# Decayed V of an attention block: built in each step from the loaded V instead of ahead of time within the MLP

## The chip, the cores and the metric

The kernel runs on one core of one Trainium2 chip. The metric is the device time of one execution in microseconds, and the median over the runs is compared.

## What is computed

The input is x of shape (4, 512, 512): 2048 tokens of width 512. Cut to what matters:

```
xn = layernorm(x)
q, k, v = xn @ wq.T, xn @ wk.T, xn @ wv.T      # 16 query heads, 4 key and value heads, head size 128
q, k = rope(q), rope(k)
s = lightning_attention(q, k, v) @ wo.T        # linear attention with decay, in chunks:
      scores = (q_i k_j) * decay(i - j);  o_intra = scores @ v
      o_inter = (q * q_decay) @ kv;       kv = blk * kv + (k * k_decay).T @ v
g = silu(mlp(xn))                              # gate, up and down, weights rounded to fp8 values
out = x + s * g
```

The kernel works with chunks of 256 tokens, so each sequence of 512 tokens has one state kv, which is made from the keys and values of its first 256 tokens and read by the queries of its last 256. It puts k_decay on V and not on K: for each of the four query heads of a group, V of the first 256 tokens is multiplied by the decay of that head. That is "decayed V". All products run in split form: every operand is a rounded part and a rest, and three products (high x high, high x low, low x high) are added.

## The kernel before, in words

There are two stages. The **MLP stage** (about the first 355 us) goes through the four sequences s = 0 to 3 in 12 slices m of the hidden width; it also makes V of all sequences (`v_tile`, `v_round`, `v_rest`), splits it and stores it to `v_dram`. The **attention stage** has 16 steps n = 4 g + b, for 4 head groups g and within each the 4 sequences b. Each engine has its own queue, written out by hand, and the engines meet at semaphores. The two middle groups are a loop (`run_steps`, L257); the last group also finishes the output (`finish`, L1020) and stores it. "Entering step n+1" below is the part of step n in which TensorE does the work for n+1 between output projections of n.

Decayed V before:

- In the MLP, VectorE adds the two parts of V again (`v_raw`, L818), multiplies by k_decay for each head (L824), ScalarE rounds the product (L537) and VectorE takes the rest (L832). There are 8 such jobs (`DECAY_JOBS`), each for four groups, so 32 blocks of 128 x 512, which SyncE stores to `vd_dram` (L323). Two halves of a small buffer (`vd_split`) alternate, so a rounding waits until the store before the last has landed (L536). Four of the jobs fetch V back first (`fetch_v`, L316).
- In the attention SyncE loads a whole step's decayed V, 1 MB, into `vd_r` (`load_vd`, L385) as soon as the last state product has read the old one.

What an attention step does around it, entering step n+1. TensorE (`projections`, L1342): key and four query projections ("tiles" 0 to 4) with output projections 0 to 2 of step n between them, then `state` (the state product: transposed key x decayed V, L1315), output projection 3, three score blocks, `inter` (L1325, queries with q_decay x state), further score blocks and the products with V (`times_v`, L1361). For tile r ScalarE copies the two halves swapped (`turn`, L616: L625, L626), VectorE multiplies by the cosine and sine tables (`rotate`, L932: L945, L946), GpSimd adds (L1142), ScalarE rounds (L614), VectorE takes the rest (`qk_rest`, L949: L952) and multiplies half of the rotated query by q_decay (`q_decay_head`, L954: L959). Between these VectorE adds up the output projections (`accumulate`, L1013). Behind all of them come ScalarE's rounding of the last q_decay block (L646), its rounding of the state (`st_round`, L635) and VectorE's `st_rest` (L969).

VectorE's queue there is:

```
for r in range(1, QK):
    rotate(n, r)
    qk_rest(n, r - 1)
    if r == 2: kn_rest(n)
    if r >= 2: q_decay_head(n, r - 2)
    for other in after.get(r, ()): other()      # accumulate (and finish) of output part r - 2
```

SyncE's queue in a step: load of decayed V, tables and weights at a group's edge, V (`load_v`, L382), xn two sequences on (`load_xn`, L395), and in the last group loads and stores of the output blocks (L398, L399, L431).

Of the kernel before, what the change touches and what calls it, by code (L numbers as in the profile page):

```python
# [11 lines left out]
P = 128  # L12
# [5 lines left out]
TT = S // P  # L18
# [47 lines left out]
DECAY_JOBS = [(2, 0), (2, 1), (0, 0), (0, 1), (1, 0), (1, 1), (3, 0), (3, 1)]  # L66
REFETCH = {2: 0, 3: 1, 4: 0, 5: 1}
VD_AT = {}
for x, t in enumerate((1, 3, 5, 7, 9, 11, 13, 15)):
    for half in range(2):  # L70
        VD_AT[2 + (t + half) // MT, (t + half) % MT] = (x, half)
# [9 lines left out]
def attention_mlp_kernel(nc, x_nat, x_t, attn_w, wv_tab, out_w, mlp_w, scales, rope_tab, decay_tab, q_decay_tab,  # L81
                         k_decay_tab, ident_in, out):
    ctx = ExitStack()
    with ctx:
# [6 lines left out]
        vd_dram = nc.dram_tensor("v_decayed", (NB, NG, P, VD, 2, S), F32, kind="Internal").ap()  # L91
# [19 lines left out]
        vd_split = sb("vd_split", [P, 2, 2, S], F32R, scope=middle)  # L111
        v_raw = sb("v_raw", [P, 2, NG, DH], scope=middle)
        vd_sb = sb("vd_sb", [P, 2, S], scope=middle)
# [34 lines left out]
        v_r = sb("v_r", [P, 2, TT, DH], F32R)  # L148
        vd_r = sb("vd_r", [P, VD, 2, S], F32R)
# [76 lines left out]
        v_out = [sem(f"v_out{i}") for i in range(VSLOT)]; v_back = [sem(f"v_back{i}") for i in range(VSLOT)]  # L226
        raw_d = sem("raw_d"); vd_m = sem("vd_m"); vd_hi = sem("vd_hi"); vd_lo = sem("vd_lo")
        vd_out = [sem("vd_out0"), sem("vd_out1")]
        v_in = sem("v_in"); vd_in = sem("vd_in"); state_d = sem("state_d")
# [41 lines left out]
        def _(sp):  # L271
# [37 lines left out]
            def fetch_v(x):  # L309
                s, j = DECAY_JOBS[x]  # L310
                r = REFETCH[x]
                sp.wait_ge(v_out[r], 32 * (3 * TT // VSLOT))
                if x >= 4:
                    sp.wait_ge(raw_d, x - 1)
                for part in range(2):
                    sp.dma_start(vs[:, r, part], v_dram[ORDER[s], :, :, part, j, :].rearrange("g p e -> p g e")).then_inc(v_back[r], 16)  # L316

            def store_vd(x, half):
                s, j = DECAY_JOBS[x]
                for g in (2 * half, 2 * half + 1):  # L320
                    y = NG * x + g
                    sp.wait_ge(vd_lo, y + 1)
                    sp.dma_start(vd_dram[ORDER[s], g, :, j], vd_split[:, y % 2].bitcast(F32)).then_inc(vd_out[y % 2], 16)  # L323

# [30 lines left out]
            for s in (2, 3):  # L355
                store_gates(s - 2)
                for m in range(MT):
                    if (s, m) in VT_AT:
                        store_v(VT_AT[s, m])
                    if (s, m) in VD_AT:  # L360
                        store_vd(*VD_AT[s, m])
                    if s == 2 and m in (3, 5, 7, 9):
                        fetch_v((m + 1) // 2)
                    if (s, m) == (2, 8):
                        spill_xn(3)
                        sp.wait_ge(ln_t, NB * TT)
                        sp.dma_start(stage[:, 0:PT, :], attn_w[0]).then_inc(aw_in, 16)
                    if (s, m) == (3, TT):
                        sp.wait_ge(vd_lo, NG * len(DECAY_JOBS))
                        sp.dma_start(rope[:], rope_tab).then_inc(rope_in, 16)  # L370
# [4 lines left out]
            for r in range(VSLOT):  # L375
                sp.wait_ge(v_out[r], 32 * (NV // VSLOT))
                sp.wait_ge(vd_out[r], 16 * (NG * len(DECAY_JOBS) // 2))
# [6 lines left out]
            def load_vd(b, g):  # L384
                sp.dma_start(vd_r[:].bitcast(F32), vd_dram[b, g]).then_inc(vd_in, 16)  # L385

            load_vd(0, 0)
# [13 lines left out]
            def group(g, final):  # L401
                for b in range(NB):
                    n = g * NB + b
                    if not (final and b == NB - 1):
                        sp.wait_ge(state_d, n + 1)
                        load_vd((b + 1) % NB, g + (b + 1) // NB)
                    if final and b == 0:
                        sp.wait_ge(gate_out, 16 * KT * NB)
                    if b == NB - 1 and not final:
                        sp.wait_ge(decayed, n * NBL + NBL)  # L410
                        load_decay(g + 1)
                    if final and b < NB - 1:
                        if b == 0:
                            sp.wait_ge(ow_lo, g * HG + HG)
                        for u in range(FINR):
                            load_fin(b, u)
                    if b == 0 and not final:
                        sp.wait_ge(ow_lo, g * HG + HG)
                        load_aw(g + 1)
                    if b == NB - 1 and not final:  # L420
                        sp.wait_ge(aw_lo, g * PT + 2 * PT)
                        sp.dma_start(stage[:, 0:HG, :], out_w[g + 1]).then_inc(ow_in, 16)
                    if not (final and b == NB - 1):
                        sp.wait_ge(d_used, n * NEL + NEL)
                        load_v((b + 1) % NB, g + (b + 1) // NB)
                    if not (final and b >= NB - 2):
                        load_xn(n + 1, (b + 2) % NB)
                    if final and b < NB - 1:
                        for u in range(KT):
                            sp.wait_ge(fin_d, b * KT + u + 1)  # L430
                            sp.dma_start(out[u, :, bass.ts(b, S)], fin[:, u % 2, :]).then_inc(stored[u % 2], 16)  # L431
                            if u + FINR < KT:
                                load_fin(b, u + FINR)
                            if b == NB - 2:
                                load_tail(u)
# [26 lines left out]
        def _(act):  # L462
# [55 lines left out]
            def v_round(v):  # L518
# [6 lines left out]
                elif v in (2 * TT + 2, 2 * TT + 3):  # L525
                    act.wait_ge(raw_d, v - 2 * TT - 1)
                elif v >= 3 * TT:
                    act.wait_ge(raw_d, v - 3 * TT + 5)
                act.copy(v_slot(v)[:, 0].bitcast(F32R), v_bank(v)[:].rearrange("p (g e) -> p g e", g=NG)).then_inc(v_hi, 1)

            def vd_round(x, half):
                for g in (2 * half, 2 * half + 1):
                    y = NG * x + g
                    act.wait_ge(vd_m, y + 1)
                    if y >= 2:
                        act.wait_ge(vd_out[y % 2], 16 * (y // 2))  # L536
                    act.copy(vd_split[:, y % 2, 0, :], vd_sb[:, y % 2, :]).then_inc(vd_hi, 1)  # L537
# [41 lines left out]
            for s in (2, 3):  # L579
                for m in range(MT):  # L580
# [4 lines left out]
                    if (s, m) in VD_AT:  # L585
                        vd_round(*VD_AT[s, m])
# [7 lines left out]
                    if s == 3 and AW_FROM <= m < AW_FROM + PT:  # L594
                        if m == AW_FROM:
                            for r in range(2):
                                act.wait_ge(vd_out[r], 16 * (NG * len(DECAY_JOBS) // 2))
# [50 lines left out]
            def projections(n, beside={}):  # L648
# [3 lines left out]
                for r in range(1, QK):  # L652
# [6 lines left out]
                    if r == 2:  # L659
                        kn_round(n)  # L660
                for other in beside.get(QK, ()):
# [59 lines left out]
        def _(dve):  # L721
# [88 lines left out]
            def vd_mult(x, half):  # L810

                s, j = DECAY_JOBS[x]
                if half == 0:
                    if x in REFETCH:
                        dve.wait_ge(v_back[x % VSLOT], 32 if x in (2, 3) else 64)
                    else:
                        dve.wait_ge(v_lo, s * TT + j + 1)
                    dve.tensor_tensor(v_raw[:, x % 2], vs[:, x % VSLOT, 0], vs[:, x % VSLOT, 1], ALU.add).then_inc(raw_d, 1)  # L818
                dve.wait_ge(raw_d, x + 1)
                for g in (2 * half, 2 * half + 1):  # L820
                    y = NG * x + g
                    if y >= 2:
                        dve.wait_ge(vd_lo, y - 1)
                    dve.tensor_tensor(vd_sb[:, g % 2, :].rearrange("p (h e) -> p h e", h=HG),  # L824
                                      v_raw[:, x % 2, g, :].unsqueeze(1).broadcast_to([P, HG, DH]),
                                      k_decay[:, g, j, :].unsqueeze(2).broadcast_to([P, HG, DH]), ALU.mult).then_inc(vd_m, 1)

            def vd_rest(x, half):
                for g in (2 * half, 2 * half + 1):
                    y = NG * x + g  # L830
                    dve.wait_ge(vd_hi, y + 1)
                    dve.tensor_tensor(vd_split[:, y % 2, 1, :], vd_sb[:, y % 2, :], vd_split[:, y % 2, 0, :].bitcast(F32),  # L832
# [71 lines left out]
            for s in (2, 3):  # L904
                for m in range(MT):
# [7 lines left out]
                    if (s, m) in VD_AT:  # L913
                        vd_mult(*VD_AT[s, m])
                    fuse(s, m)
                    if (s, m) in VD_AT:
                        vd_rest(*VD_AT[s, m])
# [54 lines left out]
            def projections(n, g, tables=None, beside={}, after={}):  # L972
# [5 lines left out]
                for r in range(1, QK):  # L978
                    for other in beside.get(r, ()):
                        other()  # L980
                    rotate(n, r)
                    qk_rest(n, r - 1)
                    if r == 2:
                        kn_rest(n)
                    if r == 2 and tables is not None:
# [185 lines left out]
        def _(pe):  # L1171
# [143 lines left out]
            def state(n):  # L1315
# [3 lines left out]
                pe.wait_ge(vd_in, n * 16 + 16)  # L1319
# [195 lines left out]
```

## Time and profile before

| | |
|---|---|
| median of 3 runs | 949.07 us (948.74 to 950.55) |
| the profiled execution | 949.77 us, span 948.0 us |
| mean granted TensorE clock | 0.989 |
| TensorE busy | 906.7 us, 96% |
| VectorE busy | 628.3 us, 66% |
| ScalarE busy | 421.3 us, 44% |
| GpSimd busy | 363.0 us, 38% |
| moved by DMA | 138.55 MB |

The span is the time from the first to the last instruction of the profiled execution; its own time is 1.8 us longer. Shares of busy time are means over both stages. TensorE's busy time is modelled and its instructions overlap, so its idle places are read from its timeline.

### The profile page before, as it was taken

How to read it: one execution, taken by the hardware profiler on the slowest of the kernel's cores; microseconds unless marked ns; L12 is line 12 of the kernel's file. 1: busy time of each engine (PE TensorE's matmuls, PEld its weight loads, DVE VectorE, ACT ScalarE, POOL GpSimd, SP SyncE). 2: the span in 40 equal slices, each digit the busy share in tenths (PEclk: the TensorE clock that was granted, in tenths of full speed). 3: DMA queues.
4: the chain of work that ended last, by engine and by line, in shares of the span. 5: the costliest groups of instructions: out<-in, count | busy, mean ns of one | idle time of the engine just before them, and what ended most of it. 6: DMA issues, size and time to landing. Idle time of an engine off the chain costs nothing.

```text
span 948.0 us, 12465 instructions
## 1 busy us (share of the span) xinstructions
PE 906.7 (96%) x4128; PEld 743.5 (78%) x4128; DVE 628.3 (66%) x915; ACT 421.3 (44%) x709; POOL 363.0 (38%) x267
## 2 busy tenths in 40 slices
PE   5799999999899999999999999999999999989996
PEld 4588888878688887888888888888888878867776
DVE  7676672676753256666787766786756677957686
ACT  3443533443532456445355445455454454533531
POOL 0011211221212475535535545455455455343541
PEclk9899999999999999999999999999999999989999
DMA  7683303468651524422333504333503333428272
GB/s 241 209 275 116 129 12 134 156 236 286 244 220 46 200 88 153 148 66 112 133 124 126 205 23 155 133 112 133 198 34 133 117 146 135 154 80 260 72 222 78
DMA packets 50971, 138.55 MB, mean 146 GB/s; under 512 B 4208, under 2 KB 25840, under 8 KB 45424
## 3 DMA queue, kind: packets, MB, share of 16 engines
q1 hardware_dynamic: 50928, 138.00, 41.9%
q8 instruction: 24, 0.39, 0.2%
q14 instruction: 19, 0.16, 0.1%
HBM read 96.04 MB, written 41.94 MB: 146 GB/s over the span
## 4 chain that ended last, share of the span: by engine, by line
PE 38%; issue 30%; POOL 19%; DVE 6%; DMA 4%; ACT 2%; SPq 1%; POOLq 0%; DVEq 0%; ACTq 0%
PE bank L1175 37%; POOL d_r L1133 11%; POOL rot L1142 8%; DMA v_decayed<-vd_split 1%; DMA out_t<-fin 1%; DMA stage<-in_x_nat 1%; DMA tail_sb<-mlp_gate 1%; ACT gout L507 1%; DVE xn L761 1%; DMA v_split<-gout 0%; DMA vs<-v_split 0%; DVE vd_split L832 0%; DVE q_r L952 0%; DVE d_sb L959 0%; PE bank L1209 0%
## 5 line engine op out<-in xcount | busy, mean ns | idle before, releaser
L1175 PE MATMUL bank<-xn,aw 128*128 128x512 f32 x960 | 228.7, 389 | 0.0
L1142 POOL TENSOR_TENSOR rot<-rot 128x512 f32<-128x512 f32 x80 | 127.8, 1598 | 237.1 <-DVE rot L946 237.1
L1175 PEld LDWEIGHTS bank<-xn,aw 128*128 128x128 f32 x960 | 179.3, 188 | 36.6
L1175 PE MATMUL bank<-xn,gu_w 128*128 128x512 f32 x768 | 183.4, 394 | 7.6 <-DVE xn L761 5.5
L1133 POOL TENSOR_TENSOR d_r<-d_sb,d_r 128x512 fp32r<-128x512 f32 x128 | 166.8, 1331 | 61.1 <-ACT d_r L646 60.9
L1175 PE MATMUL bank<-o_r,ow 128*128 128x512 f32 (+1 forms) x816 | 186.6, 379 | 0.0
L1175 PEld LDWEIGHTS bank<-xn,gu_w 128*128 128x128 f32 x768 | 145.9, 190 | 39.3 <-DVE xn L761 5.7
L1175 PEld LDWEIGHTS bank<-o_r,ow 128*128 128x128 f32 x816 | 145.7, 188 | 27.6
L646 ACT CAST d_r<-d_sb 128x512 fp32r<-128x512 f32 x128 | 78.9, 621 | 110.3 <-DVE d_sb L1004 68.8
L945 DVE TENSOR_TENSOR rot<-bank,rope 128x512 f32<-128x512 f32 x80 | 55.2, 690 | 97.1 <-ACT rot L626 96.8
L625 ACT COPY rot<-bank 64x512 f32<-64x512 f32 x80 | 46.7, 584 | 146.0 <-PE bank L1175 145.5
L1114 POOL TENSOR_TENSOR fsplit<-f_all,fsplit 128x512 fp32r<-128x512 f32 x36 | 48.4, 1350 | 133.2 <-ACT fsplit L500 133.2
L1175 PE MATMUL bank<-fsplit,dn_w 128*128 128x512 f32 x384 | 94.9, 393 | 1.1 <-ACT gout L507 0.8
L1175 PE MATMUL bank<-q_r,k_r 128*128 128x512 f32 x288 | 79.5, 402 | 8.8 <-DVE q_r L952 8.8
L1175 PEld LDWEIGHTS bank<-fsplit,dn_w 128*128 128x128 f32 x384 | 71.2, 188 | 16.5 <-issue 1.5
L1004 DVE TENSOR_TENSOR d_sb<-bank,decay 128x512 f32<-128x512 f32 x96 | 62.9, 685 | 30.1 <-PE bank L1175 27.7
L1175 PE MATMUL bank<-d_r,v_r 128*128 128x512 f32 (+1 forms) x336 | 78.5, 364 | 2.3 <-POOL d_r L1133 1.4
L959 DVE TENSOR_TENSOR d_sb<-rot,q_decay 128x256 f32<-128x256 f32 x64 | 72.6, 1134 | 0.0
L1175 PEld LDWEIGHTS bank<-d_r,v_r 128*128 128x128 f32 x336 | 57.4, 188 | 18.8 <-POOL d_r L1133 5.9
L1175 PEld LDWEIGHTS bank<-q_r,k_r 128*128 128x128 f32 x288 | 54.3, 194 | 20.7 <-DVE q_r L952 10.1
L797 DVE SCALAR_TENSOR_TENSOR f_all<-bank,scale_sb,f_all 128x512 f32<-128x512 f32 x36 | 27.0, 749 | 52.5 <-PE bank L1175 42.5
L614 ACT CAST q_r<-rot 128x512 fp32r<-128x512 f32 x64 | 39.8, 622 | 41.3 <-POOL rot L1142 40.5
(73 smaller groups left out, 949.8 us busy)
## 6 DMA issues: line engine op xcount, KB each, us to landing
xn<-xn_split SPq DMA_DIRECT2D x15, 2048.0 KB, 7.9
v_decayed<-vd_split SPq DMA_DIRECT2D x32, 512.0 KB, 3.3
vd_r<-v_decayed SPq DMA_DIRECT2D x16, 1024.0 KB, 6.8
xn_split<-xn SPq DMA_DIRECT2D x4, 2048.0 KB, 9.1
v_r<-v_split SPq DMA_DIRECT2D x16, 512.0 KB, 5.8
wst<-in_mlp_w SPq DMA_DIRECT2D x10, 768.0 KB, 5.2
stage<-in_attn_w SPq DMA_DIRECT2D x4, 1280.0 KB, 5.8
stage<-in_x_nat SPq DMA_DIRECT2D x16, 256.0 KB, 4.5
```

The lines of the kernel that those rows point to most:

```text
L507: act.activation(gout[:, d, :], down_ps[d][:], ACT.Silu, scale=scale_sb[:, 2 * MT + d:2 * MT + d + 1]).then_inc(gate_d, 1)
L614: act.copy(dst, rot1[:, r % RRING, :]).then_inc(qk_hi, 1)
L625: act.copy(rot2[0:ROT, r % RRING, :], ps[ROT:, :])
L646: act.copy(d_r[:, slot(e), 0, :], d_sb[:, slot(e), :]).then_inc(d_hi, 1)
L797: dve.scalar_tensor_tensor(out=f, in0=gu_ps[(2 * u + 1) % 3][:], scalar=scale_sb[:, MT + m:MT + m + 1], in1=f, op0=ALU.mult, op1=ALU.mult) ...
L945: dve.tensor_tensor(rot1[:, r % RRING, :], proj_bank(n, r)[:], rope[:, 0, :], ALU.mult)
L959: dve.tensor_tensor(d_sb[:, slot(e), bass.ts(h % 2, HALF)], rot1[:, (h + 1) % RRING, HALF:S], q_decay[:, h, :], ALU.mult).then_inc(q_decay ...
L1004: dve.tensor_tensor(by_head(d_sb[:, slot(e), :]), by_head(sc_ps[t % TRING][:]), decay[:, h0:h0 + nh, i0 - j:i0 - j + ni, :], ALU.mult).the ...
L1114: pool.tensor_tensor(fsplit[:, e % FRING, 1, :], src, fsplit[:, e % FRING, 0, :].bitcast(F32), ALU.subtract).then_inc(f_lo, 1)
L1133: pool.tensor_tensor(d_r[:, slot(e), 1, :], d_sb[:, slot(e), :], d_r[:, slot(e), 0, :].bitcast(F32), ALU.subtract).then_inc(d_lo, 1)
L1142: pool.tensor_tensor(rot1[:, r % RRING, :], rot1[:, r % RRING, :], rot2[:, r % RRING, :], ALU.add).then_inc(qk_sum, 1)
L1175: last = pe.matmul(dst, a, b, start=start and x == 0, stop=stop and x == len(pairs) - 1)
```

## The change

Decayed V is no longer made in the MLP, stored and loaded. Each attention step makes its own from the V that it loads anyway, in `v_r`: VectorE adds the two parts for the first 256 tokens (a sum of 256 elements a partition) and multiplies for two token tiles (512 each), after rotation 3's subtraction; ScalarE rounds the two products behind its copies for query tile 3; VectorE takes the two rests ahead of rotation 4. The state product waits for these rests and not for a load. `vd_dram`, its stores and loads, the fetches and the MLP's part are gone. The rope table's load waits for the last MLP weights instead of for decayed V.

```diff
-DECAY_JOBS = [(2, 0), (2, 1), (0, 0), (0, 1), (1, 0), (1, 1), (3, 0), (3, 1)]
-REFETCH = {2: 0, 3: 1, 4: 0, 5: 1}
...
-        vd_dram = nc.dram_tensor("v_decayed", (NB, NG, P, VD, 2, S), F32, kind="Internal").ap()
...
+        v_raw = sb("v_raw", [P, VD, DH])
+        vd_sb = sb("vd_sb", [P, VD, S])
...
-                    if (s, m) in VD_AT:
-                        store_vd(*VD_AT[s, m])
-                    if s == 2 and m in (3, 5, 7, 9):
-                        fetch_v((m + 1) // 2)
...
-                    if not (final and b == NB - 1):
-                        sp.wait_ge(state_d, n + 1)
-                        load_vd((b + 1) % NB, g + (b + 1) // NB)
...
+            def vd_round(n, j):
+                act.wait_ge(vd_m, n * VD + j + 1)
+                if_later(n, lambda: act.wait_ge(state_d, n))
+                act.copy(vd_r[:, j, 0, :], vd_sb[:, j, :]).then_inc(vd_hi, 1)
...
                     if r == 2:
                         kn_round(n)
+                    if r == 3:
+                        for j in range(VD):
+                            vd_round(n, j)
...
+            def vd_mult(n, g):
+
+                dve.wait_ge(v_in, n * 16 + 16)
+                if_later(n, lambda: dve.wait_ge(vd_lo, n * VD))
+                dve.tensor_tensor(v_raw[:], v_r[:, 0, 0:VD, :].bitcast(F32), v_r[:, 1, 0:VD, :].bitcast(F32), ALU.add).then_inc(raw_d, 1)
+                dve.wait_ge(raw_d, n + 1)
+                for j in range(VD):
+                    dve.tensor_tensor(vd_sb[:, j, :].rearrange("p (h e) -> p h e", h=HG),
+                                      v_raw[:, j, :].unsqueeze(1).broadcast_to([P, HG, DH]),
+                                      k_decay_of(g, j).unsqueeze(2).broadcast_to([P, HG, DH]), ALU.mult).then_inc(vd_m, 1)
...
+            def vd_rest(n):
+                for j in range(VD):
+                    dve.wait_ge(vd_hi, n * VD + j + 1)
+                    dve.tensor_tensor(vd_r[:, j, 1, :], vd_sb[:, j, :], vd_r[:, j, 0, :].bitcast(F32),
                                       ALU.subtract).then_inc(vd_lo, 1)
...
+                    if r == QK - 1:
+                        vd_rest(n)
                     rotate(n, r)
                     qk_rest(n, r - 1)
                     if r == 2:
                         kn_rest(n)
+                    if r == 3:
+                        vd_mult(n, g)
...
-                pe.wait_ge(vd_in, n * 16 + 16)
+                pe.wait_ge(vd_lo, n * VD + VD)
```

VectorE, entering step 1, from the rotation of query tile 3 to the one of tile 4. Before:

```order
L946 TENSOR_TENSOR rot<-rot,rope 128x512
L952 TENSOR_TENSOR q_r<-rot,q_r 128x512
L959 TENSOR_TENSOR d_sb<-rot,q_decay 128x256
L1016 COPY acc<-bank 128x512
L945 TENSOR_TENSOR rot<-bank,rope 128x512
```

After the change:

```order
L892 TENSOR_TENSOR rot<-rot,rope 128x512
L898 TENSOR_TENSOR q_r<-rot,q_r 128x512
L769 TENSOR_TENSOR v_raw<-v_r 128x256
L772 TENSOR_TENSOR vd_sb<-v_raw,k_decay 128x512 x2
L905 TENSOR_TENSOR d_sb<-rot,q_decay 128x256
L966 COPY acc<-bank 128x512
L782 TENSOR_TENSOR vd_r<-vd_sb,vd_r 128x512 x2
L891 TENSOR_TENSOR rot<-bank,rope 128x512
```

Three instructions stand between the subtraction and the q_decay product, and two between the accumulation and the rotation of tile 4; nothing else moves.

ScalarE in the same place, from the copies for tile 3. Before:

```order
L625 COPY rot<-bank 64x512
L626 COPY rot<-bank 64x512
L614 CAST q_r<-rot 128x512
L625 COPY rot<-bank 64x512
L626 COPY rot<-bank 64x512
```

After the change:

```order
L577 COPY rot<-bank 64x512
L578 COPY rot<-bank 64x512
L566 CAST q_r<-rot 128x512
L493 CAST vd_r<-vd_sb 128x512 x2
L577 COPY rot<-bank 64x512
L578 COPY rot<-bank 64x512
```

The two roundings stand ahead of the copies for tile 4.

## Rows read from the trace of the kernel before

**Rows 1.** The page, busy time, share and instructions of each engine:

```profile
PE 906.7 (96%) x4128; PEld 743.5 (78%) x4128; DVE 628.3 (66%) x915; ACT 421.3 (44%) x709; POOL 363.0 (38%) x267
```

**Rows 2.** Timeline near 242 us: start, length, engine, instruction, [idle before <-releaser]:

```profile
239.68 0.62 ACT L537 CAST vd_split<-vd_sb 128x512 fp32r<-128x512 f32 x1 [9.48 <-DMA v_decayed<-vd_split]
...
242.50 2.08 PE L1175 MATMUL bank<-xn,gu_w 128*128 128x512 f32 x8 [2.15 <-ACT f_all L491]
...
248.11 1.15 PE L1175 MATMUL bank<-fsplit,dn_w 128*128 128x512 f32 x4 [0.80 <-ACT gout L507]
```

**Rows 3.** Instructions on vd_sb: duration in ns (least/median/most), first and last start:

```profile
L824 DVE TENSOR_TENSOR vd_sb<-v_raw,k_decay x32: 677/685/1784, 168.9 to 278.1; 128x512 f32<-128x512 f32 x32
L537 ACT CAST vd_split<-vd_sb x32: 612/621/627, 169.6 to 282.2; 128x512 fp32r<-128x512 f32 x32
```

**Rows 4.** Timeline of VectorE, entering step 6:

```profile
565.22 0.68 DVE L952 TENSOR_TENSOR q_r<-rot,q_r 128x512 fp32r<-128x512 f32 x1
565.82 1.51 DVE L959 TENSOR_TENSOR d_sb<-rot,q_decay 128x256 f32<-128x256 f32 x1
...
569.54 0.69 DVE L945 TENSOR_TENSOR rot<-bank,rope 128x512 f32<-128x512 f32 x1 [1.61 <-ACT rot L626]
...
574.49 0.41 DVE L959 TENSOR_TENSOR d_sb<-rot,q_decay 128x256 f32<-128x256 f32 x1
576.14 0.69 DVE L969 TENSOR_TENSOR st_r<-bank,st_r 128x512 fp32r<-128x512 f32 x1 [1.25 <-ACT st_r L635]
```

**Rows 5.** Timelines of ScalarE, GpSimd and TensorE in the same place:

```profile
568.24 0.58 ACT L625 COPY rot<-bank 64x512 f32<-64x512 f32 x1 [3.62 <-PE bank L1175]
...
565.38 1.67 POOL L1142 TENSOR_TENSOR rot<-rot 128x512 f32<-128x512 f32 x1 [4.01 <-DVE rot L946]
570.91 1.67 POOL L1142 TENSOR_TENSOR rot<-rot 128x512 f32<-128x512 f32 x1 [3.86 <-DVE rot L946]
...
570.76 1.52 PE L1175 MATMUL bank<-vd_r,kn_r 128*128 128x512 f32 x6
...
577.06 1.69 PE L1175 MATMUL bank<-d_r,st_r 128*128 128x256 f32 x12
...
579.52 0.74 PE L1175 MATMUL bank<-d_r,v_r 128*128 128x512 f32 x2
```

**Rows 6.** Timelines entering steps 13 and 14, and a stretch's granted clock (PEclk, third last):

```profile
825.38 0.69 DVE L945 TENSOR_TENSOR rot<-bank,rope 128x512 f32<-128x512 f32 x1
826.69 1.52 PE L1175 MATMUL bank<-vd_r,kn_r 128*128 128x512 f32 x6
...
834.48 0.69 DVE L1032 TENSOR_TENSOR fin<-stage 128x512 f32<-128x512 f32 x1 [4.07 <-DMA out_t<-fin]
835.83 0.80 PE L1175 MATMUL bank<-q_r,k_r 128*128 128x512 f32 x1 [4.21 <-DVE q_r L952]
...
836.00:841.00 5.00, 5.00 (x18) 0.50 0.15 56
...
869.73 1.52 PE L1175 MATMUL bank<-vd_r,kn_r 128*128 128x512 f32 x6
...
878.91 1.16 PE L1175 MATMUL bank<-q_r,k_r 128*128 128x512 f32 x3 [4.25 <-DVE q_r L952]
```

**Rows 7.** Timelines of VectorE and TensorE, entering step 15:

```profile
909.12 0.69 DVE L1025 TENSOR_TENSOR stage<-acc,stage 128x512 f32<-128x512 f32 x1
909.85 0.69 DVE L1032 TENSOR_TENSOR fin<-stage 128x512 f32<-128x512 f32 x1
910.60 0.69 DVE L945 TENSOR_TENSOR rot<-bank,rope 128x512 f32<-128x512 f32 x1
...
911.82 1.52 PE L1175 MATMUL bank<-vd_r,kn_r 128*128 128x512 f32 x6
```

**Rows 8.** The load of V for step 8: its issue, and its time to landing:

```profile
631.10 0.33 SPq L382 DMA_DIRECT2D v_r<-v_split  x1
...
DMA to landing us min/median/max: 6.9/6.9/6.9
```

More of the change, by code:

```diff
@@ L65 @@
 VSLOT = 2
-DECAY_JOBS = [(2, 0), (2, 1), (0, 0), (0, 1), (1, 0), (1, 1), (3, 0), (3, 1)]
-REFETCH = {2: 0, 3: 1, 4: 0, 5: 1}
[L68 to L71, printed above, removed]
 AW_FROM = 6
@@ L110, in attention_mlp_kernel @@
         vs = sb("vs", [P, VSLOT, 2, NG, DH], scope=middle)
-        vd_split = sb("vd_split", [P, 2, 2, S], F32R, scope=middle)
-        v_raw = sb("v_raw", [P, 2, NG, DH], scope=middle)
-        vd_sb = sb("vd_sb", [P, 2, S], scope=middle)
         assert nc.sbuf_base <= early_end
@@ L225, in attention_mlp_kernel @@
         v_d = sem("v_d"); v_hi = sem("v_hi"); v_lo = sem("v_lo")
-        v_out = [sem(f"v_out{i}") for i in range(VSLOT)]; v_back = [sem(f"v_back{i}") for i in range(VSLOT)]
+        v_out = [sem(f"v_out{i}") for i in range(VSLOT)];
         raw_d = sem("raw_d"); vd_m = sem("vd_m"); vd_hi = sem("vd_hi"); vd_lo = sem("vd_lo")
-        vd_out = [sem("vd_out0"), sem("vd_out1")]
-        v_in = sem("v_in"); vd_in = sem("vd_in"); state_d = sem("state_d")
+        v_in = sem("v_in"); state_d = sem("state_d")
         kt_d = sem("kt_d"); kn_hi = sem("kn_hi"); kn_lo = sem("kn_lo")
@@ L307, in store_v @@
                                  v_slot(v)[:, part]).then_inc(v_out[v % VSLOT], 16)
[L309 to L323, printed above, removed]
             for i in range(TT):
@@ L368, in _ @@
                     if (s, m) == (3, TT):
-                        sp.wait_ge(vd_lo, NG * len(DECAY_JOBS))
+                        sp.wait_ge(w_ready, ready(MT - 1, down=True))
                         sp.dma_start(rope[:], rope_tab).then_inc(rope_in, 16)
@@ L376, in _ @@
                 sp.wait_ge(v_out[r], 32 * (NV // VSLOT))
-                sp.wait_ge(vd_out[r], 16 * (NG * len(DECAY_JOBS) // 2))
             sp.wait_ge(gu_done, 2 * NU)
@@ L524, in v_round @@
                     act.wait_ge(w_ready, ready(MT - 1, down=True))
[L525 to L528, printed above, removed]
                 act.copy(v_slot(v)[:, 0].bitcast(F32R), v_bank(v)[:].rearrange("p (g e) -> p g e", g=NG)).then_inc(v_hi, 1)
[L531 to L537, printed above, removed]
+            def vd_round(n, j):
+                act.wait_ge(vd_m, n * VD + j + 1)
+                if_later(n, lambda: act.wait_ge(state_d, n))
+                act.copy(vd_r[:, j, 0, :], vd_sb[:, j, :]).then_inc(vd_hi, 1)
             act.preload_act_table(ACT.Silu)
@@ L584, in _ @@
                     silu_gate(s, m)
-                    if (s, m) in VD_AT:
-                        vd_round(*VD_AT[s, m])
                     if (s, m) in VT_AT:
@@ L595, in _ @@
                         if m == AW_FROM:
-                            for r in range(2):
-                                act.wait_ge(vd_out[r], 16 * (NG * len(DECAY_JOBS) // 2))
                             for r in range(VSLOT):
@@ L808, in v_rest @@
                                   v_slot(v)[:, 0], ALU.subtract).then_inc(v_lo, 1)
[L810 to L832, printed above, removed]
+            def vd_mult(n, g):
[7 more added lines that the diff above has]
+                                      k_decay_of(g, j).unsqueeze(2).broadcast_to([P, HG, DH]), ALU.mult).then_inc(vd_m, 1)
@@ L833, in vd_rest, with k_decay_of @@
+            def k_decay_of(g, j):
+                return k_decay[:, g, j, :]
+            def vd_rest(n):
+                for j in range(VD):
+                    dve.wait_ge(vd_hi, n * VD + j + 1)
+                    dve.tensor_tensor(vd_r[:, j, 1, :], vd_sb[:, j, :], vd_r[:, j, 0, :].bitcast(F32),
                                       ALU.subtract).then_inc(vd_lo, 1)
@@ L912, in _ @@
                         inv_std(4)
-                    if (s, m) in VD_AT:
-                        vd_mult(*VD_AT[s, m])
                     fuse(s, m)
-                    if (s, m) in VD_AT:
-                        vd_rest(*VD_AT[s, m])
                     if (s, m) in VT_AT:
```

3 lines of the change are left out of this document (removed).

## The prediction

> **What bounds the kernel now.** I read the page first: TensorE is busy for 96% of the span, VectorE for 66% [rows 1]. So TensorE sets the time wherever it has no idle, and an edit elsewhere counts only through idle that it takes from TensorE or gives to it. Next I read TensorE's timeline for idle. Between 160 and 800 us it has two places that the old scheme makes, in the MLP [rows 2]; then each attention step of some 36.6 us runs almost without a gap [rows 5]; and the last group of heads has two gaps of 4.2 us that end with a store [rows 6]. (The step length is the distance of the first state product of rows 6 from that of rows 5, seven steps: (826.69 - 570.76) / 7 = 36.56.) Last I read VectorE, ScalarE and GpSimd around one step's state product, because there the new work goes.
>
> **What goes: the MLP part.** 8 sums, 32 products, 32 roundings and 32 subtractions leave the MLP, with 32 stores of 512 KB and 8 fetches of 256 KB. TensorE is full there, so most of it gives nothing. What it gives is where ScalarE stands in its queue for a store of decayed V: it waited 9.48 us for one and came late to the gate's Silu, for which TensorE idled 2.15 us, and just after that 0.80 us for the gates [rows 2]. Without those stores both waits lose their cause: **-2.95 us**. Bounds: 0 (spill and weight load keep the queue busy all the same) and -2.95. Of the 16 loads of 1 MB that leave the attention, no wait of TensorE for one is listed.
>
> **What comes: five VectorE instructions in each of 16 steps**, one sum of 256 elements, two products and two subtractions of 512, and two ScalarE roundings. The product with a broadcast operand takes 685 ns in the median, as long as any two-operand pass of 512, and a rounding 621 ns [rows 3]. Back to back, VectorE starts such passes 0.60 us apart although each is listed as 0.68 (565.22 to 565.82) [rows 4]; a wait on VectorE's own semaphore makes it 0.73 (909.12 to 909.85) [rows 7].
>
> Where they land in an ordinary step, in the order of VectorE's queue. After the subtraction at 565.22 stood the 256-element product with q_decay, 1.51 us long, where the same form takes 0.41 at 574.49 [rows 4]: GpSimd's add runs from 565.38 to 567.05 [rows 5], and the product gets through when it ends. Now the sum v_raw stands there and takes over that wait, and ends at the same 567.25. What is added is therefore the start distances of the rest: 0.13 (semaphore) + 2 x 0.60 (products) + 0.33 (the q_decay product, now not held) + 2 x 0.60 (subtractions ahead of the fourth query's rotation) = **2.86 us**. I take 0.33 as 0.41 less the overlap of 0.08 that the other passes have. VectorE stood idle for 1.61 us before that rotation (569.54) [rows 4], 1.69 counted from start to start. So the rotation starts 2.86 - 1.69 = **1.17 us later**, at 570.7. ScalarE's side agrees: its two roundings run from 568.1 to 569.3, so its two copies of the fourth query start at 569.3 in place of 568.24 [rows 5] and are done at about 570.5, just before.
>
> Who waits for that: behind the rotation stand GpSimd's add, the last subtraction, the last q_decay product, ScalarE's rounding of it, and behind that in ScalarE's queue the rounding of the state, then st_rest at 576.14, which ends 0.23 us before TensorE's inter-chunk products begin at 577.06; from st_rest the chain goes on through the first decay block, ScalarE and GpSimd to the first product with V at 579.52 [rows 4, 5]. That chain is already tight, so it hands on 1.0 to 1.17 us. The state product itself (570.76) waits only for the two new subtractions, done at 570.8, 0.1 us. I take **1.2 us a step** for the steps whose chain looks like this: the twelve transitions into steps 1 to 12. For step 0, where the same passes lie among the last down projections and ScalarE's new roundings stand ahead of a rounding that GpSimd and TensorE want, no row measures the wait; I price it as one more step, bounds 0 and 3. 13 x 1.2 = **+15.6 us**. Bounds per step: 0.9 (0.3 us of slack I have not seen) and 1.6 (one wait of GpSimd more is shared).
>
> V itself comes earlier in demand than before: a step's V load used to be needed by the products with V, now by v_raw. The tightest ordinary case issues it at 631.10 and it lands 6.9 us later, at 638.0 [rows 8]; v_raw of that step would start as in the step shown, 4.9 us before its state product, which by two step lengths comes at 570.76 + 2 x 36.56 = 643.9; so v_raw wants it at 639.0. It fits by 1 us, so I price it at 0.
>
> **The last group.** Entering steps 13 and 14 TensorE idles 4.21 and 4.25 us until the last query's subtraction, which stands behind a `finish` that waits 4.07 us for an output store [rows 6]. That store is issued behind the load of xn, so its time does not depend on VectorE. VectorE has no idle before the rotation there (825.38, no idle noted), so it is 2.86 us late, at 828.2; its new subtractions end at 828.3 and the state product of 826.69 waits 1.6 us. But the store lands when it did, so the step ends when it did: 4.21 is divided into 1.6 and 2.6. That has a consequence. After the first long gap the granted clock stood at 0.50, TensorE's 1.2 GHz level [rows 6], and the two steps are 43.04 and 42.09 us long; less 36.56 and less the gap that leaves 2.27 and 1.28 us that the low clock costs. After the gap of 2.15 us the eight products took 2.08 us, the full rate [rows 2]. 2.6 is nearer to 2.15 than to 4.2, so I take it that the clock stays up: **-3.55 us**, bounds 0 and -3.55. Entering step 15 the store is no longer what ends last and VectorE has no idle at all from 909.12 on [rows 7], so its 2.86 us come through nearly whole; some 0.2 us less because loads of gates land earlier without the 1 MB ahead of them: **+2.7**, bounds 1.5 and 3.5.
>
> **Sum.** -2.95 + 15.6 + 2.7 - 3.55 = +11.8 us on the profiled execution's 949.77, that is 961.6. The median of the runs shown, 949.07, lies 0.70 below that execution, so I forecast 961 (960.9).
>
> **A rule against the change.** All five new passes read both operands from SBUF, and the row of 1.51 against 0.41 us shows what that can cost beside a GpSimd instruction. The Trainium skill (SBUF — State Buffer, on the engine ports) says that such a pass and a GpSimd instruction take an exclusive lock on a shared pair of ports, and the loser waits for the whole instruction. The trace agrees (565.82 to 567.33, GpSimd's end 567.05). By that rule alone one could charge every new pass with such a wait; the sum charges none, because the first takes over a wait that was there and the others meet an idle GpSimd. The skill's page VectorE: DVE Perf Modes (The DRAIN you can't avoid) lets the next pass start only when the pipe is empty; by full durations the five passes and the wait would be 2.86 + 4 x 0.08 = 3.2 us, and a step 1.5 in place of 1.2. The row's start distance of 0.60 decides for me.
>
> **Rivals.**
> 1. *The low clock comes all the same* in steps 13 and 14: against it only the one gap of 2.15 us. 961 + 3.55 = 964.5.
> 2. *Passes and GpSimd collide once more in each step*: the products slip into GpSimd's next add or delay it. One more hold costs 1.51 - 0.41 = 1.1 us, 13 times: 961 + 14 = 975. For it: the row of 1.51. Against: after its add GpSimd idles 3.86 us, until 570.91 [rows 5].
> 3. *The cover holds and the kernel is faster.* The mechanism is VectorE's idle before the fourth query's rotation, 1.69 us. If the added start distances are below 1.69 us, the rotation is on time, and only the MLP's 2.95 us are left: 949.07 - 2.95 = 946. That needs 1.2 us of my 2.86 to be hidden, such as the sum and the products running while GpSimd adds; the held q_decay product speaks against it.
> 4. *V lands late* in the six steps at a group's edge or start: with 1 to 2 us each, 961 + 9 = 970.
> 5. *The products are not what the code says*, or the wait is not on the way: nothing for it; the order of instructions shows all five in each step.
>
> **Chances.** Forecast 0.48 (with bounds 955 to 967), rival 1 0.25, rival 2 0.10, rival 4 0.08, rival 3 0.06, others 0.03. The range 953 to 970 takes in the forecast's bounds, rival 1 and rival 4, and leaves out rivals 2 and 3. A difference of 0.2% (1.9 us) is what measurement can tell from none; faster by more than that is rival 3 and a bit, 0.07; within it 0.04; slower 0.89.
>
> **What would show it.** In the changed kernel's trace: no idle of 2 us on TensorE near 242 us; rotation of the fourth query right behind vd_rest, without VectorE idle; an idle of about 1 us on TensorE before the inter-chunk products in steps 1 to 12, and steps of 37.7 us; in steps 13 and 14 one idle before the state product and one of 2.6 before the second score block, with the granted clock at 1.00 after it. Wrong would be: steps of 36.5 us (cover held), steps of 39 (contention), or VectorE idle ahead of v_raw for a load.

## The result and the profile after the change

The changed kernel takes 964.57 us (median of 4 runs, 963.62 to 965.39), the kernel before on the same chip 949.81 us (948.74 to 950.55). The ratio is 1.0156, with a 95% interval of 1.0138 to 1.0174: 14.8 us slower. Its profiled execution takes 965.39 us with a span of 963.6, so it stands 0.8 us above its median; spans differ by 15.6 us.

The page of the changed kernel, part 1 (busy time of each engine) and the DMA total:

```profile
PE 912.2 (95%) x4128; PEld 738.6 (77%) x4128; DVE 602.5 (63%) x923; ACT 422.4 (44%) x709; POOL 363.5 (38%) x267
...
DMA packets 39834, 102.89 MB, mean 107 GB/s; under 512 B 3312, under 2 KB 20848, under 8 KB 36336
```

By totals this looks better than [rows 1]: VectorE is busy 26 us less and 35.7 MB fewer are moved. Both were taken from places where nobody waited for them. What matters is where the rest of VectorE's work now stands.

TensorE's timeline near 242 us, where before there were two waits [rows 2] (columns: start, length, engine, instruction, and in brackets idle before and what ended it):

```profile
236.71 1.98 PE L1125 MATMUL bank<-fsplit,dn_w 128*128 128x512 f32 x8
238.52 3.79 PE L1125 MATMUL bank<-xn,gu_w 128*128 128x512 f32 x16
242.15 2.88 PE L1125 MATMUL bank<-wv,xn 128*128 128x512 f32 x12
244.87 1.29 PE L1125 MATMUL bank<-fsplit,dn_w 128*128 128x512 f32 x5
```

No idle is left; the down projections that began at 248.11 begin at 244.87, **3.24 us earlier**.

VectorE's timeline, entering step 6, to be held beside [rows 4]:

```profile
570.31 0.69 DVE L898 TENSOR_TENSOR q_r<-rot,q_r 128x512 fp32r<-128x512 f32 x1
570.92 1.51 DVE L769 TENSOR_TENSOR v_raw<-v_r 128x256 f32<-128x256 f32 x1
572.46 1.29 DVE L772 TENSOR_TENSOR vd_sb<-v_raw,k_decay 128x512 f32<-128x512 f32 x2
573.67 0.42 DVE L905 TENSOR_TENSOR d_sb<-rot,q_decay 128x256 f32<-128x256 f32 x1
574.01 0.69 DVE L968 TENSOR_TENSOR acc<-bank,acc 128x512 f32 x1
574.61 1.28 DVE L782 TENSOR_TENSOR vd_r<-vd_sb,vd_r 128x512 fp32r<-128x512 f32 x2
575.81 0.69 DVE L891 TENSOR_TENSOR rot<-bank,rope 128x512 f32<-128x512 f32 x1
...
577.61 0.42 DVE L905 TENSOR_TENSOR d_sb<-rot,q_decay 128x256 f32<-128x256 f32 x1
...
582.56 0.69 DVE L915 TENSOR_TENSOR st_r<-bank,st_r 128x512 fp32r<-128x512 f32 x1 [1.25 <-ACT st_r L587]
```

The sum v_raw has the 1.51 us that the q_decay product had, and that product is back at 0.42. Ahead of the rotation (575.81) no idle is noted any more. Behind that rotation something else has changed, too: the q_decay product of 577.61 takes 0.42 us, while before, in the same place, it was held as well:

```profile
571.35 1.51 DVE L959 TENSOR_TENSOR d_sb<-rot,q_decay 128x256 f32<-128x256 f32 x1
```

ScalarE, GpSimd and TensorE in the same place of the changed kernel, beside [rows 5]:

```profile
573.18 1.23 ACT L493 CAST vd_r<-vd_sb 128x512 fp32r<-128x512 f32 x2 [3.46 <-DVE vd_sb L772]
574.43 0.58 ACT L577 COPY rot<-bank 64x512 f32<-64x512 f32 x1
575.03 0.58 ACT L578 COPY rot<-bank 64x512 f32<-64x512 f32 x1
...
577.17 2.01 POOL L1092 TENSOR_TENSOR rot<-rot 128x512 f32<-128x512 f32 x1 [5.03 <-DVE rot L892]
...
575.95 1.67 PE L1125 MATMUL bank<-vd_r,kn_r 128*128 128x512 f32 x6
...
583.48 0.74 PE L1125 MATMUL bank<-d_r,st_r 128*128 128x256 f32 x4 [0.78 <-POOL d_r L1083]
```

Counted from the state product, st_rest began 5.38 us after it and now begins 6.61 us after it; TensorE's products with the state began 6.30 after it and now 7.53, with an idle of 0.78 us that was not there. The state products of steps 1 to 12 are 37.6 to 38.3 us apart, before 36.3 to 36.9.

TensorE in the last group, entering steps 13 and 14, beside [rows 6]:

```profile
843.10 1.60 PE L1125 MATMUL bank<-vd_r,kn_r 128*128 128x512 f32 x6 [1.47 <-DVE vd_r L782]
...
850.63 1.65 PE L1125 MATMUL bank<-q_r,k_r 128*128 128x512 f32 x6 [2.53 <-DVE q_r L898]
...
884.73 1.66 PE L1125 MATMUL bank<-vd_r,kn_r 128*128 128x512 f32 x6 [1.47 <-DVE vd_r L782]
...
892.20 2.10 PE L1125 MATMUL bank<-q_r,k_r 128*128 128x512 f32 x6 [2.40 <-DVE q_r L898]
894.64 2.58 PE L1125 MATMUL bank<-d_r,st_r 128*128 128x256 f32 x12 [0.34 <-POOL d_r L1083]
```

Each gap of 4.2 us is now one before the state product and one before the second score block. After the first the products run at full rate (six in 1.65 us), after the second they don't.

### The profile page after: what moved, and what is told of

Read it like the earlier page. It is cut to its first block, busy times and chain, and to the rows that moved or that the text cites. A ratio compares the mean times of both kernels' runs of the same rounds, so it can differ in the third digit from the quotient of the medians.

```text
span 963.6 us, 12451 instructions
## 1 busy us (share of the span) xinstructions
PE 912.2 (95%) x4128; PEld 738.6 (77%) x4128; DVE 602.5 (63%) x923; ACT 422.4 (44%) x709; POOL 363.5 (38%) x267
## 4 chain that ended last, share of the span: by engine, by line
PE 37%; issue 31%; POOL 19%; DVE 6%; DMA 2%; ACT 2%; POOLq 0%; SPq 0%; DVEq 0%; ACTq 0%
PE bank L1125 37%; POOL d_r L1083 10%; POOL rot L1092 9%; DMA out_t<-fin 1%; DVE rot L891 1%; DVE q_r L898 1%; DMA tail_sb<-mlp_gate 1%; DVE xn L716 0%; DMA v_split<-gout 0%; DVE v_raw L769 0%; DMA stage<-in_x_nat 0%; DVE rot L892 0%; PE bank L1159 0%; DVE d_sb L954 0%; DVE vd_sb L772 0%
## 5 line engine op out<-in xcount | busy, mean ns | idle before, releaser
L1092 POOL TENSOR_TENSOR rot<-rot 128x512 f32<-128x512 f32 x80 | 132.0, 1650 | 258.0 <-DVE rot L892 258.0
L1083 POOL TENSOR_TENSOR d_r<-d_sb,d_r 128x512 fp32r<-128x512 f32 x128 | 164.5, 1309 | 54.9 <-ACT d_r L598 54.7
L1125 PEld LDWEIGHTS bank<-xn,gu_w 128*128 128x128 f32 x768 | 145.9, 190 | 36.9 <-DVE xn L716 5.7
L1125 PEld LDWEIGHTS bank<-q_r,k_r 128*128 128x128 f32 x288 | 52.0, 189 | 22.3 <-DVE q_r L898 12.7
L898 DVE TENSOR_TENSOR q_r<-rot,q_r 128x512 fp32r<-128x512 f32 x64 | 52.9, 826 | 15.7 <-ACT q_r L566 15.3
```

What stands on the lines that cost most here:

```text
L898: dve.tensor_tensor(dst, rot1[:, r % RRING, :], hi.bitcast(F32), ALU.subtract).then_inc(qk_lo, 1)
L1083: pool.tensor_tensor(d_r[:, slot(e), 1, :], d_sb[:, slot(e), :], d_r[:, slot(e), 0, :].bitcast(F32), ALU.subtract).then_inc(d_lo, 1)
L1092: pool.tensor_tensor(rot1[:, r % RRING, :], rot1[:, r % RRING, :], rot2[:, r % RRING, :], ALU.add).then_inc(qk_sum, 1)
L1125: last = pe.matmul(dst, a, b, start=start and x == 0, stop=stop and x == len(pairs) - 1)
```

## The experiments

Each is compared with the kernel before in its own rounds: 948.28 us for the first four, 948.48 for the last four.

**The MLP part alone.** The kernel before, without its work on decayed V in the MLP.

```diff
-                    if (s, m) in VD_AT:
-                        store_vd(*VD_AT[s, m])
...
-                sp.dma_start(vd_r[:].bitcast(F32), vd_dram[b, g]).then_inc(vd_in, 16)
+                for j in range(VD):
+                    sp.dma_start(vd_r[:, j].bitcast(F32), v_dram[b, g].rearrange("p a t e -> p a (t e)")).then_inc(vd_in, 16)
...
-                        vd_mult(*VD_AT[s, m])
```

> The kernel before without the MLP's work on decayed V; the attention still loads 1 MB per step into the same place (V's own bytes, so the state is computed from wrong values) and VectorE and ScalarE do nothing new there. My sum: the two waits at 242 us (2.15 + 0.80 us) go and nothing else, 946.9 us against 949.8, attention steps of 36.4 to 36.6 us. Rival: the 16 MB of stores and the fetches cost more than these two waits (contention for the DMA engines over 120 us of the MLP): 942 or less. Other rival: spill and weight loads keep the wait, 949.8.

Measured: 944.99 us, ratio 0.9967 (0.9958 to 0.9977), so 3.3 us less, between 2.2 and 4.0. The attention steps 1 to 12 are 36.3 to 36.9 us long, as before. The gain of the MLP is these two waits; 18.9 MB less through the DMA engines in the MLP give nothing beside them that could be measured.

**The attention part alone.** The kernel before with its MLP untouched, and with the new work in each step in place of the loads of decayed V.

```diff
-                    if not (final and b == NB - 1):
-                        sp.wait_ge(state_d, n + 1)
-                        load_vd((b + 1) % NB, g + (b + 1) // NB)
...
+                    if r == 3:
+                        vd2_mult(n, g)
...
-                pe.wait_ge(vd_in, n * 16 + 16)
+                pe.wait_ge(vd2_lo, n * VD + VD)
```

> The kernel before with its whole MLP work and stores kept, and in the attention the new per-step work in place of the 1 MB loads. My sum: the changed kernel's 964.6 plus the 2.95 us of the MLP = 967.5 us, steps of 37.75 us. Rival (the two parts are not additive, the MLP part hides elsewhere): 964.6.

Measured: 968.03 us, ratio 1.0213 (1.0197 to 1.0228). Ordinary steps (those that neither begin nor end a head group) are 37.6 to 37.9 us. The parts add, as far as can be told: 19.8 - 3.3 = 16.5 against 14.8 us for both together, and the 1.7 us that are over lie within the intervals (18.7 to 21.6, 2.2 to 4.0 and 13.1 to 16.5 us). In the profiled execution the clock takes some of it, as TensorE's timeline shows after the MLP's wait:

```profile
242.18 2.74 PE L1199 MATMUL bank<-xn,gu_w 128*128 128x512 f32 x8 [2.04 <-ACT f_all L487]
```

Eight products took 2.74 us behind an idle of 2.04, where the kernel before took 2.08 behind 2.15 [rows 2]; the granted clock stood at 0.50 from 244 to 246 us, and again from 855 to 857 us, entering step 13. In the changed kernel it fell only entering step 14.

**Without the sum.** The products read V's rounded part.

```diff
-                dve.tensor_tensor(v_raw[:], v_r[:, 0, 0:VD, :].bitcast(F32), v_r[:, 1, 0:VD, :].bitcast(F32), ALU.add).then_inc(raw_d, 1)
-                dve.wait_ge(raw_d, n + 1)
...
-                                      v_raw[:, j, :].unsqueeze(1).broadcast_to([P, HG, DH]),
+                                      v_r[:, 0, j, :].bitcast(F32).unsqueeze(1).broadcast_to([P, HG, DH]),
```

> The changed kernel without the sum of V's two parts; the products read V's rounded part alone. Theory (VectorE's start distances beyond its idle of 1.69 us before the rotation of tile 4 set the step): the first product takes over the wait for GpSimd, what goes is the sum's own 0.33 and the semaphore's 0.13, less 0.03: 0.43 us a step, 14 steps, 958.5 us, steps of 37.3. Rival (ScalarE's roundings in front of its copies for tile 4 set it): the copies start when TensorE's projection and the roundings are done, at most 0.2 us earlier: 962. Rival (each two-operand pass pays GpSimd's lock): 1.5 us a step, 944.

Measured: 957.29 us, ratio 1.0098 (1.0083 to 1.0114), ordinary steps of 37.2 to 37.3 us. VectorE's timeline:

```profile
565.73 0.68 DVE L896 TENSOR_TENSOR q_r<-rot,q_r 128x512 fp32r<-128x512 f32 x1
566.33 2.37 DVE L770 TENSOR_TENSOR vd_sb<-v_r,k_decay 128x512 f32<-128x512 f32 x2
568.63 0.41 DVE L903 TENSOR_TENSOR d_sb<-rot,q_decay 128x256 f32<-128x256 f32 x1
```

Two products take 2.37 us from their start where they took 1.29: the first now waits for GpSimd's add. From the subtraction to the q_decay product it is 2.90 us, in the changed kernel 3.36 (570.31 to 573.67): 0.46 us less in VectorE's queue, and about 0.5 us less in the step. Whoever stands first behind rotation 3's subtraction pays GpSimd, once. The steps and the total came out as the theory had them (37.3 and 958.5 us).

**Sum and products ahead of rotation 3.**

```diff
+                    if r == 3:
+                        vd_mult(n, g)
                     if r == QK - 1:
                         vd_rest(n)
...
-                    if r == 3:
-                        vd_mult(n, g)
```

> The changed kernel with sum and products ahead of the rotation of tile 3 in place of behind its subtraction. Theory (idle before rotations is the cover): in the six ordinary steps 1.66 us of work fits into 1.76 us of idle before rotation 3, and the two rests into the 1.69 before rotation 4, so these steps fall to 36.5; in the three steps at a group's end there is no idle before rotation 3 and V has not landed, they stay 1.5 to 2 us longer; in those after a group's start V lands about when it is wanted, 1 us longer. Together 953 to 956 us. Rival (the added work itself costs, wherever it stands): 964.6 unchanged. Rival (V's landing holds the queue up at the earlier place in every step): above 966.

Measured: 958.55 us, ratio 1.0112 (1.0096 to 1.0127): 4.5 us better than the changed kernel, not the 9 to 12 that I expected. VectorE entering step 7, an ordinary step:

```profile
599.40 0.41 DVE L769 TENSOR_TENSOR v_raw<-v_r 128x256 f32<-128x256 f32 x1
599.84 1.29 DVE L772 TENSOR_TENSOR vd_sb<-v_raw,k_decay 128x512 f32<-128x512 f32 x2
601.27 0.69 DVE L891 TENSOR_TENSOR rot<-bank,rope 128x512 f32<-128x512 f32 x1
...
605.11 1.28 DVE L782 TENSOR_TENSOR vd_r<-vd_sb,vd_r 128x512 fp32r<-128x512 f32 x2
606.79 0.69 DVE L891 TENSOR_TENSOR rot<-bank,rope 128x512 f32<-128x512 f32 x1 [0.41 <-ACT rot L578]
```

All five passes are there, and 0.41 us of idle is left before the rotation of tile 4; the steps whose entry looks like this are 36.4 to 36.5 us long (459.76 from 423.34, 608.02 from 571.56). So the work costs nothing where idle covers it. That holds entering steps 2, 3, 6, 7, 10 and 11; entering steps 1, 4, 5, 8 and 12, at a group's edge, VectorE again has no idle before the rotation of tile 4 and the chain still comes about 1 us later (1 to 2 were expected), entering step 9 0.3 us. The miss lies in the last group, where V's load stands behind 1.5 MB of loads for the output. VectorE and TensorE entering step 13:

```profile
825.91 0.43 DVE L769 TENSOR_TENSOR v_raw<-v_r 128x256 f32<-128x256 f32 x1 [2.71 <-DMA v_r<-v_split]
...
834.30 2.31 PE L1125 MATMUL bank<-vd_r,kn_r 128*128 128x512 f32 x6 [3.86 <-DVE vd_r L782]
```

VectorE's queue stands 2.71 us for V and TensorE 3.86 us for the state's operand, and the low clock follows (six products in 2.31 us, before 1.52). The same comes twice more. I had seen that V would be late at a group's edge and had not asked it of the last group.

**Two and five spare passes in the kernel before.** VectorE multiplies tables that nobody reads, ahead of the rotation of tile 4; for the second kernel 5 stands for 2.

```diff
+                    if r == QK - 1:
+                        for x in range(2):
+                            dve.tensor_tensor(spare[:, x, :], q_decay[:, 0:2, :], q_decay[:, 2:4, :], ALU.mult)
                     rotate(n, r)
```

> The kernel before with two spare VectorE products of 512 (operands in SBUF, nobody waits for them) ahead of the rotation of tile 4 in each step. Theory: 1.2 us of start distances stay below the idle of 1.69 us, steps stay at 36.4 to 36.6; only entering step 15, where VectorE has no idle, 1.2 us show: 949.5 us against 948.3. Rival (any added VectorE work costs its length, since the chain through the rotation is tight): 1.2 us a step, 965.

Measured: 950.16 us, ratio 1.0019 (1.0009 to 1.0028). The steps are 36.3 to 36.9 us up to step 13, and VectorE keeps 0.41 of its 1.61 us of idle. Entering step 15, where it has none, TensorE idles 1.99 us before a score block (0.36 in the kernel before). VectorE's timeline in an ordinary step:

```profile
567.11 1.28 DVE L984 TENSOR_TENSOR spare<-q_decay 128x512 f32<-128x512 f32 x2
568.80 0.69 DVE L946 TENSOR_TENSOR rot<-bank,rope 128x512 f32<-128x512 f32 x1 [0.41 <-ACT rot L627]
```

> The same with five spare products, 3.0 us. Theory: 3.0 - 1.69 = 1.3 us a step for entering steps 1 to 12, steps of 37.8 as in the changed kernel although ScalarE and GpSimd have nothing new to do; entering step 15 3.0 us; entering steps 13 and 14 hidden behind the store. 948.3 + 15.7 + 3 = 967, less up to 3.5 if the low clock stays away. Rival (ScalarE's roundings or the shared port make the changed kernel's steps long, VectorE alone does not): at most 955.

Measured: 972.61 us, ratio 1.0247 (1.0230 to 1.0265). Ordinary steps are 37.8 to 37.9 us, which is the changed kernel's length, with no new work on ScalarE or GpSimd and no load that anybody waits for. So VectorE's queue alone is enough to make the steps that long. GpSimd's add behind the rotation takes 2.01 us and the q_decay product 0.41 here, too. The total is 5.6 us above my 967. The largest part comes from entering step 0, which I had left out of the expectation; TensorE there:

```profile
351.83 5.53 PE L1179 MATMUL bank<-fsplit,dn_w 128*128 128x512 f32 x16 [2.37 <-POOL fsplit L1118]
```

Idle 2.37 us for GpSimd and then sixteen products in 5.53 us where the changed kernel takes 3.92; the state product of step 0 starts at 357.20, before at 354.40. Also each step costs 1.48 us (417.81 between the state products of steps 1 and 12, before 401.55) and not 1.3.

**The output store ahead of the load of xn**, in the kernel before, for steps 12 and 13.

```diff
+                    if final and b < NB - 2:
+                        store_out(b, 0)
                     if not (final and b >= NB - 2):
                         load_xn(n + 1, (b + 2) % NB)
```

> The kernel before with one thing moved: in the last group SyncE issues the first output store of steps 12 and 13 ahead of the 2 MB load of xn. Theory (the gaps of 4.2 us end with that store, and it is queued behind xn): both waits of 4.07 us go, TensorE's gaps fall to 0.2 to 1 us and the granted clock stays up: 948.3 - 8.1 - 3.5 = 937 us. Rival (the loads of gates and x, not the store, hold finish up): 948.

Measured: **941.02 us, ratio 0.9913 (0.9896 to 0.9929)**. SyncE's queue and TensorE entering step 13:

```profile
819.87 0.34 SPq L403 DMA_DIRECT2D out_t<-fin  x1
824.37 0.33 SPq L395 DMA_DIRECT2D xn<-xn_split  x1
...
831.99 1.65 PE L1181 MATMUL bank<-q_r,k_r 128*128 128x512 f32 x6 [0.17 <-DVE q_r L958]
834.19 1.69 PE L1181 MATMUL bank<-d_r,st_r 128*128 128x256 f32 x12 [0.55 <-DVE st_r L975]
```

The gap of 4.21 us is 0.17, the six products run at full rate, and the steps from 13 to 15 take 37.61 and 37.86 us instead of 43.04 and 42.09. This beats both kernels. The gain is 7.5 us and not the 11.6 expected, because behind the store VectorE, which has no idle there, is next: 0.55 to 0.9 us before the products with the state in these steps, 1.39 us before a score block entering step 15. In the profiled executions the state product of step 15 comes 9.5 us earlier, the end 8.5.

**Early products up to step 12, late ones in the last group, and the store edit**, in the changed kernel.

```diff
+                last_group = isinstance(g, int) and g == NG - 1
...
+                    if r == 3 and not last_group:
+                        vd_mult(n, g)
...
+                    if r == 3 and last_group:
                         vd_mult(n, g)
```

> The changed kernel with sum and products ahead of rotation 3 in all steps but those of the last group, where they stay behind its subtraction, and with the first output store ahead of xn as in the run of that edit alone. Theory: steps up to 12 as in the run with early products (11.1 us less than the changed kernel up to the state product of step 12), no wait for V in the last group, and 3 to 4 us less from the store: 948.3 + 14.8 - 11.1 - 3.5 = 948.5 us. Since VectorE has no idle in the last group, it cannot reach the kernel before with the same store edit. Rival (V's landing in the last group holds it up in this order too): 955.

Measured: 951.53 us, ratio 1.0025 (1.0015 to 1.0034). The state product of step 12 comes at 793.58, 10.2 us earlier than in the changed kernel. From the state product of step 12 on, the steps are 39.2, 40.3 and 40.6 us, where the store edit on the kernel before has 36.5, 37.6 and 37.9; TensorE:

```profile
832.76 1.62 PE L1134 MATMUL bank<-vd_r,kn_r 128*128 128x512 f32 x6 [1.47 <-DVE vd_r L788]
...
838.92 1.67 PE L1134 MATMUL bank<-q_r,k_r 128*128 128x512 f32 x6 [1.12 <-DVE q_r L904]
```

There VectorE has no idle to cover anything, so the five passes are paid nearly in full, 2.7 us in each of these steps. 11.7 us of the changed kernel's 14.8 go with order alone, but most of that is the store's, which the kernel before can have as well: with the same store edit in both, the kernel before takes 941.02 us and this one 951.53, so the change still costs 10.5 us and the order of the products has taken off about 4. The remainder needs work taken off VectorE in the last group, which wasn't tried.

## Why the prediction was right, and where it was off

The forecast was 961 us in 953 to 970 and slower with 0.89; measured 964.57, 14.8 us above the kernel before where the sum said 11.8. That the time is also what rival 1 gave (964.5) is chance: only about half of rival 1 came true, and the steps made up the rest. By the prediction's own steps, on the profiled executions:

- **The MLP, -2.95.** Right, 0.3 beyond its bound: 3.24 us by the timeline, 3.3 alone on the chip (2.2 to 4.0). ScalarE's wait for the store of decayed V was the cause.
- **The place and the cover, 2.86 - 1.69 = 1.17 us.** The rotation of tile 4 began 1.22 us ahead of the state product and now begins 0.14 us ahead of it, so it is 1.08 later against a product that is itself held for a tenth. Two spare passes fit into the idle and five don't, and both came out at the computed place. The sum takes over the wait for GpSimd, as said. V was never late up to step 12: no wait of v_raw for it is noted there.
- **1.2 us a step.** Under-sized. The state products of steps 1 and 12 are 416.77 us apart (387.00 and 803.77), before 401.55 (388.64 and 790.19): 15.2 us in 11 steps, **1.38 us** each. Most of the missing 0.2 us lies on GpSimd's side. Entering step 6, counted from the start of TensorE's projection for tile 4 (565.32, now 570.42), the rotation comes 1.17 us later, which is the computed figure. GpSimd's add behind it took 2.01 us where it took 1.67 [rows 5], with the q_decay product beside it 0.42 where it took 1.51, so the add ends 1.50 us later. The last query's subtraction waits for that add through ScalarE; 0.2 us come back on the way, and st_rest and TensorE's products with the state are 1.32 us later. The run with the early products has entries with the rotation in the same place, 0.13 us ahead of the state product, in which the two meet as before. GpSimd, VectorE and TensorE there, entering step 5:

```profile
535.31 1.67 POOL L1092 TENSOR_TENSOR rot<-rot 128x512 f32<-128x512 f32 x1 [3.36 <-DVE rot L892]
535.75 1.51 DVE L905 TENSOR_TENSOR d_sb<-rot,q_decay 128x256 f32<-128x256 f32 x1
541.47 1.68 PE L1125 MATMUL bank<-d_r,st_r 128*128 128x256 f32 x12 [0.79 <-POOL d_r L1083]
```

  TensorE's products with the state begin 7.39 us after the state product (534.08), in the changed kernel 7.55 us after it entering the same step: 0.16 us for the longer add. I had moved the whole chain by the rotation's delay and not asked whether the two engines would still meet in the same order. Why they don't, no run shows: it isn't VectorE's missing idle, which is missing here as well.
- **Step 0, priced as one more step.** Right in size: the state product of step 0 comes 1.82 us earlier where the MLP gave 3.24, so 1.42 us. TensorE idles 0.46 and 1.02 us there for GpSimd, before 0.32 us.
- **The last group, -3.55 + 2.7.** The division of the gap was right: 1.47 and 2.53 us where I had 1.6 and 2.6. The clock was half right: entering step 13 it stayed up, entering step 14 it fell. The granted clock of the two places (columns: stretch, its length, TensorE busy, granted clock, DMA share, GB/s):

```profile
851.00:852.00 1.00, 1.00 (x6) 1.00 0.57 219
...
894.00:895.00 1.00, 0.66 (x2) 0.50 0.00 0
```

  So rival 1, the low clock all the same, came true for one of two. Entering steps 13 and 15 VectorE also waited 0.65 and 0.73 us for V (rival 4 in small), mostly in place of the wait for GpSimd. In all the last group cost 0.8 us (what the other terms leave of 15.6), where the sum had -0.85.
- **Sum.** MLP -3.2, entering steps 0 to 12 1.42 + 12 x 1.38 = +18.0 (forecast 15.6), last group +0.8 (forecast -0.85): +15.6 on the spans. The 2.4 us of the steps and the 1.6 of the last group are the miss.
- **The two rules.** A hold for each new pass did not show. Behind rotation 3 there is one, as before, and the run without the sum shows it moving to whichever pass stands first, which fits an exclusive lock. The Trainium skill (SBUF — State Buffer, SBUF: two separate sides) gives the shared ports to whichever of the two instructions starts first, and blocks the other. Behind rotation 4 there were 1.51 us before and up to step 12 there are none; GpSimd's add is 0.34 us longer instead. This other direction, GpSimd held by VectorE, is what I left out; by the listed starts the add is first in both kernels. Nor did full durations show: the two products and the one with q_decay start 1.21 us apart (572.46 to 573.67), 0.60 us for each.

Rival 2 (one more hold of 1.1 us a step) and rival 3 (cover holds) fall with the steps of 37.7 us; of rival 2's mechanism, passes that delay GpSimd's add, a seventh of its price is real. Rival 3's mechanism is real, though: with the passes spread over two idles, the same work is free in ordinary steps.

What stays open: what decides whether VectorE's product or GpSimd's add gets through first, what decides the clock after a gap of 2 to 2.5 us, and whether a V load ahead of the output loads would make the early order work in the last group.

## What to carry to other kernels

An engine at 66% can be the one that decides: look at the idle right ahead of the instruction that a tight chain hangs on, count added work in start distances, and compare the two; here 1.2 us were free and 2.86 cost 1.4 in every step. Work moved from a stage with hardly any waiters into a chain with waiters gains nothing by being less in total. And when a stall is found on the way (an output store queued behind a 2 MB load), try its repair by itself: it was worth twice what the MLP gave.

## What the runs showed of the hardware that was not expected

- Idle times of TensorE of nearly the same length ended at either clock. At full rate afterwards: 2.15 us (before, MLP), 2.22 (store first, MLP), 2.42 (attention part alone, step 14), 2.53 (after, step 13). At the low level: 1.99 and 2.03 (two spare passes, step 15 and MLP), 2.04 and 2.37 (attention part alone, MLP and step 13), 2.37 (five spare passes, step 0), 2.40 (after, step 14). So in this range the length of a gap did not say what it costs, and a term like my -3.55 should be given as a range.
- Which of VectorE's q_decay product and GpSimd's add gets through first can be read neither from their listed starts (the product's is 0.44 us behind the add's in either case) nor from VectorE's idle. With idle ahead of the rotation of tile 4 the product took 1.51 us and the add 1.67 (kernel before). Without idle it was 0.42 and 2.01 entering steps 1 to 12 of the changed kernel, but 1.51 and 1.67 entering its steps 13 to 15 and wherever the run with early products had none.
